# An accumulating GpSimd transfer issued one step later, between two elementwise operations, from two buffers; one buffer of values fewer

## What is computed

```
x = x + 0.5 * ffn(layernorm(x), w_router, w1, w2, w3)
x = x + attention(layernorm(x), Wq, Wk, Wv, Wo, omega, mu, sigma, ...)
x = x + 0.5 * ffn(layernorm(x), w_router, w1, w2, w3)
```

```
maha   = max(qn_i + E*E*kn_j - 2*E*s_ij, 0) / V_ij
logits = coef * log(1 + maha / nu) - 0.5 * DH * log(V_ij)      (causal)
A      = softmax(logits);   out = (A @ v) of all heads;   y = out @ Wo
```

## Time and profile before

| | |
|---|---|
| median of three runs | 1673.64 us |
| profiled execution | 1672.11 us |
| its span | 1670.2 us |
| TensorE busy | 97% of the span |
| VectorE busy | 87% |
| ScalarE busy | 86% |
| GpSimd busy | 67% |

### The profile page before, as it was taken

One profiled execution on the slowest core, in us unless ns is written; L12 is line 12 of the kernel. 1 busy time (PEld: TensorE's weight loads), 2 busy tenths in 40 slices (PEclk: granted clock), 3 DMA queues, 4 the chain that ended last, 5 costly groups with the idle time before them and its releaser, 6 DMA issues. The chain is left out here.

```text
span 1670.2 us, 30882 instructions
## 1 busy us (share of the span) xinstructions
PE 1616.2 (97%) x9690; PEld 1228.9 (74%) x9690; DVE 1457.7 (87%) x3020; ACT 1443.9 (86%) x2909; POOL 1116.1 (67%) x1074
## 2 busy tenths in 40 slices
PE   5999988999999999999999999999999999899998
PEld 4787865777777777777777777777777776677876
DVE  6878888899899989999998998999899889967665
ACT  6677778999999999999999999999999999775765
POOL 3554556778668767776877787777777677245555
PEclk9999999999999999999999999999999999999999
DMA  6000023444444444444443544354454433000000
GB/s 179 1 1 1 1 92 80 89 118 91 112 96 108 100 100 107 94 113 92 111 101 89 123 95 103 80 124 101 99 115 88 111 83 75 22 7 7 14 13 13
DMA packets 67761, 131.49 MB, mean 79 GB/s; under 512 B 10128, under 2 KB 27792, under 8 KB 67600
## 3 DMA queue, kind: packets, MB, share of 16 engines
q1 hardware_dynamic: 50320, 98.07, 22.9%
q0 software_dynamic: 17280, 31.46, 10.9%
HBM read 17.95 MB, written 5.24 MB: 14 GB/s over the span
## 5 line engine op out<-in xcount | busy, mean ns | idle before, releaser
L1501 POOL TENSOR_TENSOR early<-early 128x1024 f32<-128x1024 f32 x127 | 303.3, 2388 | 305.2 <-PE pS L1192 164.4
L661 POOL TENSOR_TENSOR hid_lo_d<-hid_d,hid_hi_d 128x512 fp32r<-128x512 f32 x176 | 231.4, 1315 | 218.8 <-ACT hid_hi_d L566 213.2
L1192 PE MATMUL pS<-early 128*128 128x128 f32 (+3 forms) x1024 | 297.6, 433 | 0.4 <-PEq L115 0.4
L1377 ACT ACTIVATE early<-early,nmax 128x128 f32<-128x128 f32 (+3 forms) x512 | 281.0, 558 | 13.0 <-DVE nmax L1588 13.0
L1393 ACT ACTIVATE early<-early,qnorm 128x128 f32<-128x128 f32 (+3 forms) x512 | 246.7, 553 | 48.5 <-DVE early L1601 47.6
L1597 DVE SCALAR_TENSOR_TENSOR pS<-pS,ek 128x1280 f32<-128x1280 f32 x128 | 191.7, 1498 | 73.6 <-PE pS L1192 72.2
L1192 PEld LDWEIGHTS pS<-early 128*128 128x128 f32 x1024 | 164.7, 191 | 96.1 <-issue 61.4
L1510 POOL TENSOR_TENSOR ek<-early 128x128 f32<-128x128 f32 (+3 forms) x256 | 215.8, 871 | 3.0 <-ACT early L1385 2.5
L1510 POOL TENSOR_TENSOR ek<-decay,early 128x128 f32<-128x128 f32 (+3 forms) x256 | 214.7, 866 | 0.0
L1406 ACT ACTIVATE early<-early,params 128x512 f32<-128x512 f32 (+1 forms) x256 | 196.5, 816 | 0.0
L1234 PE MATMUL pS<-ident,early 128*128 128x128 f32 x1280 | 182.0, 278 | 6.9 <-DVE early L1601 4.5
(11 more groups left out here) (395 smaller groups left out, 3836.5 us busy)
## 6 DMA issues: line engine op xcount, KB each, us to landing
early<-early SPq DMA_DIRECT2D x263, 256.0 KB, 3.5
x_sb<-weighed POOLq DMA_DIRECT2D x120, 256.0 KB, 4.2
early<-trig_d SPq DMA_DIRECT2D x64, 64.0 KB, 2.4
trig_d<-early SPq DMA_DIRECT2D x3, 1024.0 KB, 7.0
early<-in_w SPq DMA_DIRECT2D x3, 704.0 KB, 8.6
x_sb<-in_x SPq DMA_DIRECT2D x4, 512.0 KB, 8.3
early<-in_wqk SPq DMA_DIRECT2D x16, 128.0 KB, 3.4
cos<-trig_d SPq DMA_DIRECT2D x32, 64.0 KB, 2.6
```

Of the source, the lines that this page charges most:

```text
L661: g.tensor_tensor(hid_lo[:, par], hid[:, par], hid_hi[:, par].bitcast(F32), ALU.subtract).then_inc(lo_done, 1)
L1192: last = pe.matmul(s.pS[:, span(I)], rot[:, I * P:(I + 1) * P], rot[:, N:N + (I + 1) * P], start=True, stop=True)
L1377: last = a.activation(z[:, span(I)], z[:, span(I)], ACT.Exp, bias=nmax[:, I:I + 1], scale=-1.0, accum_out=rsum[:, r % 4, I:I + 1])
L1501: g.tensor_tensor(rot[:], by_cos[:], crossed[:], ALU.add).then_inc(S["rot_done"], 1)
```

## The change

The accumulation's place in GpSimd's program moves: in step r it was made last, for pair r-3; now it is made between the rotation and the spread of r+1, for pair r-4, so one step later. `weighed` becomes two buffers, used by even and odd pairs, with a semaphore each, so that L1626 waits for the transfer two pairs back. The memory for the second buffer comes from `val_even`, which has two buffers now; the copy at L1419 waits for the weighing two pairs back.

```diff
-        weighed = sb("weighed", [P, TILES, P])
+        weighed = [sb(f"weighed{k}", [P, TILES, P]) for k in range(2)]
-        val_even = [sb(f"val_even{k}", [P, N]) for k in range(3)]
+        val_even = [sb(f"val_even{k}", [P, N]) for k in range(2)]
+        acc_done = (S["acc_done0"], S["acc_done1"])
@@ TensorE, weigh
-                val = val_even[r % B % 3] if parity(r) == 0 else val_odd[r % B]
+                val = val_even[r % B % 2] if parity(r) == 0 else val_odd[r % B]
@@ ScalarE, values_out
-                if live(i, r - 3):
-                    wait(a, S["av_done"], i * 16 + r - 2)
-                for h, val in enumerate((val_even[r % B % 3], val_odd[r % B])):
+                if live(i, r - 2):
+                    wait(a, S["av_done"], i * 16 + r - 1)
+                for h, val in enumerate((val_even[r % B % 2], val_odd[r % B])):
@@ GpSimd, accumulate and a_step
-                g.dma_start(xb, weighed[:], accum_op=ALU.add).then_inc(S["acc_done"], 16)
+                g.dma_start(xb, weighed[n % 2][:], accum_op=ALU.add).then_inc(acc_done[n % 2], 16)
                         rotate(i, r + 1)
+                if live(i, r - 4) and n - 4 < (H - 1) * B:
+                    accumulate(i, r - 4)
+                if live(i, r + 1):
                     spread(i, r + 1)
                     query_norms(i, r + 1)
-                if live(i, r - 3) and n - 3 < (H - 1) * B:
-                    accumulate(i, r - 3)
@@ VectorE, normalise_out
-                    v.wait_ge(S["acc_done"], 16 * (n - B + 1))
+                    v.wait_ge(acc_done[n % 2], 16 * ((n - B) // 2 + 1))
-                wait(v, S["acc_done"], 16 * n)
-                v.tensor_tensor(weighed[:], s.p7.rearrange("p (c d) -> p c d", c=TILES),
+                wait(v, acc_done[n % 2], 16 * (n // 2))
+                v.tensor_tensor(weighed[n % 2][:], s.p7.rearrange("p (c d) -> p c d", c=TILES),
```

More of the change, by code:

```diff
@@ L1847, in program @@
                  "ek_done s_done w_done t_done relu_done ln_done zred_done exp_done v_done "
-                 "y_done qt_done val_done tr_done trc_done av_done rinv_done acc_done stat_done dve_passed pool_passed sp_passed "
+                 "y_done qt_done val_done tr_done trc_done av_done rinv_done acc_done0 acc_done1 stat_done dve_passed pool_passed sp_passed "
                  "late_stat late_mv late_var late_ln late_root late_rstd late_step late_xn late_xt late_hi late_lo mv_done expanded0 expanded1")
```

## The result

The changed kernel takes 1699.93 us (median of 4 runs, 1698.88 to 1700.70), the kernel before beside it on the same chip 1674.13 us: the ratio is 1.0156, with a 95% interval of 1.0141 to 1.0172. The direction was forecast, the size was not: 26 us instead of 16. The time lies at the upper edge of the stated range (1674 to 1700 us) and above that of case A (1682 to 1697 us), for which the sum stood. The span of the profiled execution grows from 1670.2 to 1698.8 us, by 28.6 us, at nearly the same granted clock (0.999, and 0.998 before).

The account below looks back on a forecast made before the run. TensorE was taken to bound both kinds of step, with VectorE 0.09 us short of it in odd ones. 14.6 + 3 - 2 = +16 us on 1672.1 gave 1688, and 1.5 us for the median gave 1690; range 1674 to 1700.

Parts of the forecast that it names:

- case A: The forecast itself: odd steps 0.28 us longer through overlap of spread and peaks; 1690 us, own range 1682 to 1697, chance 0.66.
- The move out of the old place: Taking the accumulation from ahead of GpSimd's next rotation, where its issue lay inside waiting time anyway: gain 0.
- the two buffers of values: ScalarE's copy waits for the same step's weighing: cost 0, or 10 us without the cover before TensorE's norms.
- the price of overlap: What VectorE's peaks lose beside GpSimd's spread in odd steps: 0.20 us at 0.40 us of overlap, then slope 0.62.
- d: Lengthening of one odd step: 0.28 us, between 0 and 0.50, in 52 steps 14.6 us.
- The feedback: An odd step longer by d puts the next peaks d later against the spread, so the overlap is 1.28 - d.
- crossed transfer at no cost: The accumulation, issued some 2.2 us ahead of the second crossed half, doesn't delay it: 0, upper estimate 0.3 us a step.
- The 2 us for the wait of `weighed`: Two buffers remove VectorE's 1.9 us of waiting for the accumulation's landing: -2 us.
- the +3 us for the late landings: Ten odd steps behind late crossed transfers lose 0.88 us and the step behind nothing, instead of 2 x 0.28: +3 us.
- B: Full exclusion in odd steps: each microsecond of overlap costs VectorE a whole one, d = 0.49; 1700 us, chance 0.14.
- C: VectorE's peaks take the port between GpSimd's spread products, GpSimd waits, d = 0; not slower, 1672 us, chance 0.13.
- D: Late crossed landings come from the accumulation issued behind them and vanish with it; faster, 1664 us, chance 0.07.

Follow-up runs that it names:

- run 1: Changed kernel with the accumulation put back last, behind the query norms, buffers and later pair kept: 1676.65 us, ratio 1.0007 to the kernel before.
- run 7: Changed kernel with a GpSimd product between accumulation and spread: over 128 columns 1723.86 us; over 4 columns, its end waited for, 1706.77 us.
- run 6: Changed kernel accumulating one token tile of four, rotation also waiting for VectorE's peaks: 1695.37 us. Its text also chains two rules through the changed kernel's steps.
- run 3: Changed kernel whose spread writes constants by memset and reads nothing, instead of its four products: 1665.72 us (one run).
- run 2: Kernel before with two buffers of even-head values and a 512-column GpSimd product between rotation and spread, accumulation left last: 1694.04 us, ratio 1.0101.
- run 4: Changed kernel without any accumulation in the first 15 heads: 1669.31 us, ratio 0.9964 to the kernel before.
- run 5: Changed kernel accumulating one token tile of four, GpSimd held as long but the transfer short: 1718.22 us, ratio 1.0243 to the kernel before.

## Why the prediction was off

**Right: where it happens and how.** The spread ends 0.87 us later (0.88 booked), even steps stay at 9.87 but for two, the loss sits in VectorE's first peaks in the odd steps, TensorE's transposes wait for VectorE, and the wait of `weighed` vanishes. The move out of the old place gained nothing, and the two buffers of values cost nothing (run 1).

**Wrong: the price of overlap.** This is the step that failed first of all. I had drawn a line between the earlier trace rows (0.20 us at 0.40) and the earlier trace rows (0.67 at 1.16) and read a slope of 0.62 from it. There is no such slope. The price is the overlap less 0.19 us, and in the kernel before the steps with 0.94 us and more lose 0.28 us less, VectorE getting one peak in between two products; the line joined the two pieces. The rows had the hint: from the earlier trace rows the price rises one for one, 0.47 us for 0.46. And behind an issue the step of 0.28 us is missing (run 7), which no row of before could show. With the right price the prediction's own sum reads 8.46 + d = 8.17 + (1.28 - d) - 0.19, so d = 0.40 instead of 0.28. Over 52 steps that is 6 us more than booked. Run 6 (`peaks_first`) has 0.41 over the kernel before; that it is so close is in part luck, since that kernel has a wait more and two landings more beside a code transfer.

The feedback was right, but it does not settle. A step that loses much leaves the next one little overlap: 0.07 and 0.71 us of excess follow each other in the windows above, and so on down the run. With a price of one for one the steps swing between the two, and the mean of such a pair is d. But a run of seven steps begins with a long one and so has four long and three short ones: the chain of run 6 with every landing at 3.73 us gives 23.1 us in 51 steps, 0.45 a step, where the prediction had 14.6.

**Wrong: crossed transfer at no cost.** I took 0, since the accumulation would be well ahead, and gave 0.3 us a step (6 us) as the upper end. The crossed halves do land later, at 4.10 instead of 3.79 us in the odd steps without a code transfer. By the chain in run 6 that is worth 2.8 us, where the upper end was 6; the difference of 5.5 us there holds more than that. My argument looked at the accumulation's landing; the delay goes with how far ahead its issue is (run 3), and in long steps the lead shrinks.

**Small terms.** The 2 us for the wait of `weighed` did not show (ratio 1.0007 in run 1). Of the +3 us for the late landings little shows: chained with the kernel before's own landings, the two rules of run 6 give 33.9 us, 23.7 more than that kernel's 10.2, and 23.1 without any late landing. The first step's 1.5 us was not foreseen, and is not the place's.

**The rivals.** A's mechanism with B's time: 1700 us was B's figure, from a price without the free 0.19 us (d = 0.49), with the +3 and -2 us that did not show and with no term for the accumulation beside the crossed halves. The price is nearly right; that it met the time to the microsecond is luck. Of B's statement, that a microsecond of overlap costs a whole one, the traces leave all but those 0.19 us standing. The Trainium skill (SBUF — State Buffer, section "Who interferes with whom") calls the shared port pair an exclusive lock; the changed kernel's trace agrees (overlap plus 1.78 us at every overlap), and I should have weighed it above two points on a line. C (GpSimd gives way between products) exists in the kernel before and in runs 2 and 7, but it is worth 0.28 us, not the whole loss, and it does not happen behind an issue. D fell with run 4.

## What to carry over

Where two engines exclude each other, take the price of overlap as one for one until two rows on the same side of an instruction's edge say otherwise: a line through points on both sides of an edge mixes two regimes. Work that is moved on GpSimd is not priced by the time that it holds GpSimd alone, but by which of VectorE's two-input instructions the work behind it now meets, and a step that is made longer there can meet the next block of GpSimd's work as well. A transfer that is moved near another one needs its own price by the distance of their issues.

## What the runs showed of the hardware

- GpSimd products behind a transfer's issue without a wait have records that overlap (4.43 us inside 3.58), and VectorE waits out all that are left, up to 2.55 us for a 0.35 us instruction. Behind a wait they are 3.5 us inside 3.40, and VectorE gets one peak in between at overlaps of 0.94 to 1.96 us, two from 2.49 us on (run 7). A memset in their place costs VectorE nothing at 0.87 us (run 3).
- An accumulating transfer issued 0.7 us ahead of a transfer inside SBUF comes with a landing after 5.5 us instead of 3.8 (run 3); at 2.2 us ahead it is 4.0, at 3.1 us 3.8 to 3.9. With a quarter of the bytes it is 3.8 to 3.95 even at 1.1 to 1.2 us ahead (run 5).
- Two collisions in a row are far more than twice one: the step of 14.69 us has 6.2 us of excess. By an estimate from its records it lost about 2 us to the spread (2.55 instead of 0.35 us), 2.1 to the rotation (2.58 instead of 0.47), and the other 2 to TensorE's clock, which fell to 0.50 during 3.64 us of idling (the weighing took 3.92 us instead of 2.39).
